# Stage one of a fused token-mixing kernel: three fp32r products in place of one fp32 product, with transfers that convert and add

## The reference, cut to what matters

```python
h = einsum('bhid,oi,od->bho', x, weighted_sum, weight)   # stage one: x is (4, 512, 256, 4)
h = concatenate([h, txt], axis=1)                        # 512 + 77 rows of 256 per batch
xn = layernorm(h)
hid = relu(xn @ gate_w1 + gate_b1); gate = sigmoid(hid @ gate_w2 + gate_b2)
glob = gate * (xn @ U_w) * cumsum(xn @ V_w, axis=1)
h = h + conv3(xn, conv_w) + glob @ out_w + out_b         # conv3: three taps along the rows
y = layernorm(h)
q = round(y / (absmax(y)/127)); qr = round(rhs / (absmax(rhs)/127))
h = h + (q @ qr) * scales                                # int8 product, exact in bf16
```

## Time and profile before

| | |
|---|---|
| three runs | 127.47 us median (126.95 to 129.34) |
| profiled execution, its own time | 126.82 us |
| its span, first to last instruction | 125.0 us |
| mean granted TensorE clock | 0.983 |

### The profile page before, as it was taken

The page is one execution under the profiler, slowest core; times in us unless marked ns, Lnnn a source line. Parts: engine busy times, 40 slices in busy tenths (PEclk is TensorE's granted clock), DMA queues, the critical chain, the costliest instruction groups (busy, mean ns, idle before and its releaser), DMA issues.

```text
span 125.0 us, 1954 instructions
## 1 busy us (share of the span) xinstructions
PE 113.8 (91%) x612; PEld 92.6 (74%) x612; DVE 83.3 (67%) x258; ACT 60.6 (49%) x132; POOL 49.5 (40%) x91
## 2 busy tenths in 40 slices
PE   6999999999999999999889999998996379999960
PEld 5678887687886986888478868866783267999830
DVE  0443431857449688867969898599689948548862
ACT  1300456644814395566048491934484856342520
POOL 2000430022002556362546737360947364554740
PEclk9999999999999999999999999999999959999998
DMA  3899999980000000000012000002021002111014
GB/s 85 237 360 336 423 419 419 419 341 13 0 0 0 0 5 0 3 0 0 33 50 84 5 28 0 0 0 87 0 84 30 0 0 84 39 45 30 3 36 157
DMA packets 5307, 12.05 MB, mean 96 GB/s; under 512 B 456, under 2 KB 3632, under 8 KB 4529
## 3 DMA queue, kind: packets, MB, share of 16 engines
q1 hardware_dynamic: 4721, 11.27, 24.5%
q10 hardware_dynamic: 576, 0.66, 1.7%
HBM read 9.52 MB, written 2.41 MB: 95 GB/s over the span
## 4 chain that ended last, share of the span: by engine, by line
PE 78%; DVE 13%; ACT 3%; issue 2%; POOL 1%; POOLq 0%; ACTq 0%; DVEq 0%
PE h_ps L720 42%; PE uvg_ps L778 5%; PE xt_ps L847 4%; PE h_ps L806 4%; PE h_ps L810 4%; DVE csum L601 3%; PE qt_ps L829 3%; DVE convT L613 3%; PE acc_ps L840 3%; DVE tmp L679 2%; PE uvg_ps L785 2%; DVE stats L552 2%; PE h_ps L816 2%; PE xt_ps L764 2%; ACT qT L488 1%
## 5 line engine op out<-in xcount | busy, mean ns | idle before, releaser
L720 PE MATMUL h_ps<-w_tok,x_sb 128*128 128x256 f32 x256 | 64.2, 394 | 0.0
L720 PEld LDWEIGHTS h_ps<-w_tok,x_sb 128*128 128x128 f32 x256 | 48.0, 197 | 9.5 <-issue 3.6
L552 DVE BATCH_NORM_STATS2 stats<-h_ps 128x6 f32<-128x256 f32 (+1 forms) x36 | 13.9, 423 | 13.9 <-PE h_ps L816 7.8
L341 POOL TENSOR_SCALAR rstd<-mv 128x2 f32<-128x2 f32 (+2 forms) x21 | 4.8, 227 | 37.4 <-DVE mv L555 36.7
L379 POOL TENSOR_SCALAR v<-xc,qmul 128x256 f32<-128x256 f32 (+1 forms) x20 | 10.6, 538 | 16.0 <-DVE qmul L657 15.8
L342 POOL TENSOR_TENSOR rstd<-rstd,exponent 128x2 f32<-128x2 f32 (+2 forms) x21 | 15.0, 713 | 1.8
L481 ACT ACTIVATE glob<-glob 32x256 fp32r<-32x256 f32 (+1 forms) x16 | 7.2, 448 | 11.9 <-POOL glob L353 6.3
L505 ACT ACTIVATE xc<-h_ps,nmean 128x256 f32<-128x256 f32 (+1 forms) x20 | 8.6, 470 | 8.9 <-DVE nmean L629 8.9
L353 POOL TENSOR_TENSOR glob<-gate,us 32x256 f32<-32x256 f32 x8 | 6.6, 831 | 14.7 <-ACT gate L472 14.7
L495 ACT ACTIVATE xn<-h_ps,shift,rstd 128x256 f32<-128x256 f32 x16 | 8.2, 564 | 8.7 <-DVE shift L641 8.6
L391 POOL TENSOR_TENSOR fin<-tmp,h 128x512 f32<-128x512 f32 (+1 forms) x10 | 11.0, 1100 | 0.5 <-DVE tmp L679 0.5
(11 more groups left out here) (89 smaller groups left out, 147.5 us busy)
## 6 DMA issues: line engine op xcount, KB each, us to landing
x_sb<-x_dram SPq DMA_DIRECT2D x6, 1024.0 KB, 16.1
out_dram<-fin SPq DMA_DIRECT2D x8, 256.0 KB
x_sb<-x_dram SPq DMA_DIRECT2D x2, 512.0 KB, 8.5
x_sb<-x_dram SPq DMA_DIRECT2D x2, 256.0 KB, 5.7
txt_sb<-txt_dram SPq DMA_DIRECT2D x1, 308.0 KB
out_dram<-fin SPq DMA_DIRECT2D x4, 77.0 KB
par_sb<-par_dram SPq DMA_DIRECT2D x1, 277.0 KB, 9.1
ws_sb<-ws_dram ACTq DMA_DIRECT2D x2, 128.0 KB, 4.2
```

What stands on the lines that cost most here:

```text
L552: last = nc.vector.bn_stats(stats[0:rows, t, :], src(t))
L720: last = nc.tensor.matmul(h_of(g)[:, t, :], x_sb[:, g, kc, t * P:(t + 1) * P], w_tok[:, kc, :], start=(kc == 0 and t == 0), stop=(kc == KC ...
```

## The change

Groups 0 and 1 stay as they are. For groups 2 to 7 a k step is six fp32r matmuls of 128 x 256: high part of x times high part of w, high x times low w, low x times high w, for each half of the rows. The high part of x comes from a transfer that GpSimd issues and that converts fp32 to fp32r; ScalarE copies its negative into `x_low`; a second GpSimd transfer adds x to that in place. Both are in halves of 512 KB, so each group takes four transfers and two copies. Three buffers go round. `w_high` is made by ScalarE, `w_low` by VectorE. The first loads are spread anew over the SyncE and ScalarE queues, x of group 0 has its own layout, and w's rows are spread by eight transposes in place of four matmuls. `nmean` goes: `centre` makes the negative of the centred value from the mean directly; `scale` loses its use of `rstd2`, which a product in `out` takes in.

```diff
+PLAIN = 2
+RING = 3
+HIGH_AT = {2: 0, 3: 0, 4: 0, 5: 25, 6: 33, 7: 41}
+NEGATE_AT = {2: (0, 1), 3: (9, 11), 4: (20, 22), 5: (30, 32), 6: (38, 40), 7: (46, 48)}
...
-WARM_FIRST = 3
+WARM_FIRST = 4
...
-            eng.dma_start(x_sb[:, g, k, :], x[g, :, k, :]).then_inc(x_loaded[g][n], 16)
+            src = x[g - 1, :, k, :] if g else x0[k, :, :].rearrange("k p t -> p k t")
+            eng.dma_start(x_sb[:, g, k, :], src).then_inc(x_loaded[g][n], 16)
...
+        HALF_KC = [slice(0, KC // 2), slice(KC // 2, KC)]
+
+        def turn_of(g):
+            return 16 * ((g - PLAIN) // RING + 1)
...
-            sp.dma_start(wt_sb[:, :], wt).then_inc(wt_loaded, 16)
-            load_x(sp, 0, 0)
-            load_x(sp, 0, 2)
-            load_x(sp, 0, 4)
+            for n in range(len(LOADS[0]) - 1):
+                load_x(sp, 0, n)
             load_x(sp, 1, 0)
             sp.dma_start(txt_sb[:, :, :], txt.rearrange("b t d -> t b d")).then_inc(txt_loaded, 16)
             load_x(sp, 1, 1)
             sp.dma_start(par_sb[:, :], par).then_inc(par_loaded, 16)
             sp.dma_start(rhs_sb[:, :, :], rhs).then_inc(rhs_loaded, 16)
-            for g in range(2, GROUPS):
-                load_x(sp, g, 0)
...
+            def load_high(g):
+                if g == PLAIN:
+                    pool.wait_ge(x_loaded[1][1], 16)
+                if g >= PLAIN + RING:
+                    pool.wait_ge(tok_done, g - RING + 1)
+                for n, k in enumerate(HALF_KC):
+                    nc.gpsimd.dma_start(x_high[:, g % RING, k, :], x[g - 1, :, k, :]).then_inc(high_loaded[g % RING][n],
+                                                                                            16)
+
+            def add_x(g, n):
+                pool.wait_ge(negated, 2 * (g - PLAIN) + n + 1)
+                nc.gpsimd.dma_start(x_low[:, g % RING, HALF_KC[n], :], x[g - 1, :, HALF_KC[n], :],
+                                    accum_op=ALU.add).then_inc(low_ready[g % RING][n], 16)
+
             for tick in range(TICKS):
+                for g in range(PLAIN, GROUPS):
+                    if tick == HIGH_AT[g]:
+                        load_high(g)
+                for g in range(PLAIN, GROUPS):
+                    for n in range(2):
+                        if tick == NEGATE_AT[g][n] + 1:
+                            add_x(g, n)
...
-            act.dma_start(ws_sb[:, 0, :], ws[:, 0, :]).then_inc(ws_loaded[0], 16)
-            load_x(act, 0, 1)
-            load_x(act, 0, 3)
-            act.dma_start(ws_sb[:, 1, :], ws[:, 1, :]).then_inc(ws_loaded[1], 16)
-
+            act.dma_start(wt_sb[:, :], wt).then_inc(wt_loaded, 16)
+            for c in range(CB):
+                act.dma_start(ws_sb[:, c, :], ws[:, c, :]).then_inc(ws_loaded[c], 16)
+            act.wait_ge(x_loaded[0][-1], 16)
             act.wait_ge(ones_ready, 1)
...
+            for n, k in enumerate(HALF_KC):
+                act.wait_ge(w_tok_ready, (n + 1) * KC // 2)
+                nc.scalar.activation(w_high[:, k, :], w_tok[:, k, :], ACT.Copy).then_inc(w_high_ready, 1)
+
+            def negate(g, n):
+                act.wait_ge(high_loaded[g % RING][n], turn_of(g))
+                if g >= PLAIN + RING:
+                    act.wait_ge(tok_done, g - RING + 1)
+                nc.scalar.activation(x_low[:, g % RING, HALF_KC[n], :], x_high[:, g % RING, HALF_KC[n], :], ACT.Copy,
+                                     scale=-1.0).then_inc(negated, 1)
...
-                    act.wait_ge(nmean2_ready, j + 1)
+                    act.wait_ge(var2_ready, j + 1)
...
-                                                    ACT.Identity, bias=nmean2[0:rows, j, t:t + 1])
+                                                    ACT.Identity, scale=-1.0, bias=mv2[0:rows, j, t, 0:1])
...
+                for g in range(PLAIN, GROUPS):
+                    for n in range(2):
+                        if tick == NEGATE_AT[g][n]:
+                            negate(g, n)
...
+            for n, k in enumerate(HALF_KC):
+                dve.wait_ge(w_high_ready, n + 1)
+                nc.vector.tensor_tensor(w_low[:, k, :], w_tok[:, k, :], w_high[:, k, :].bitcast(F32),
+                                        ALU.subtract).then_inc(w_low_ready, 1)
...
-                    dve.wait_ge(var2_ready, j + 1)
-                    nc.vector.tensor_scalar(nmean2[0:rows, j, 0:nt], mv2[0:rows, j, 0:nt, 0], -1.0, None,
-                                            ALU.mult).then_inc(nmean2_ready, 1)
...
-                    dve.wait_ge(rstd2_ready, j + 1)
-                    for t in range(nt):
-                        last = nc.vector.tensor_scalar(ls[:, t:t + 1], a[:, t:t + 1], rs[:, t:t + 1], SCALE_FLOOR,
-                                                       ALU.mult, ALU.max)
-                    then_wait(last)
-                    then_wait(nc.vector.reciprocal(a, ls))
-                    nc.vector.scalar_tensor_tensor(out=qm, in0=a, scalar=INT8_MAX, in1=rs, op0=ALU.mult,
-                                                   op1=ALU.mult).then_inc(qmul_ready, 1)
+                    then_wait(nc.vector.tensor_scalar(am, a, SCALE_FLOOR * LN_EPS ** 0.5, -1.0 / INT8_MAX,
+                                                      ALU.max, ALU.mult))
+                    nc.vector.reciprocal(qm, am).then_inc(qmul_ready, 1)
...
+                    dve.wait_ge(rstd2_ready, j + 1)
+                    then_wait(nc.vector.tensor_tensor(lscale[0:rows, j, 0:nt], nstep[0:rows, j, 0:nt],
+                                                      rstd2[0:rows, j, 0:nt], ALU.mult))
...
+                    if kc % (KC // 2) == 0:
+                        pe.wait_ge(high_loaded[g % RING][kc // (KC // 2)], turn_of(g))
+                        pe.wait_ge(low_ready[g % RING][kc // (KC // 2)], turn_of(g))
+                    if g == PLAIN and kc == 0:
+                        pe.wait_ge(w_high_ready, 2)
+                        pe.wait_ge(w_low_ready, 2)
+                    for t in range(2):
+                        at = slice(t * P, (t + 1) * P)
+                        nc.tensor.matmul(h_of(g)[:, t, :], x_high[:, g % RING, kc, at], w_high[:, kc, :],
+                                         start=(kc == 0 and t == 0), stop=False, skip_group_check=True)
+                        nc.tensor.matmul(h_of(g)[:, t, :], x_high[:, g % RING, kc, at], w_low[:, kc, :],
+                                         start=False, stop=False, skip_group_check=True)
+                        last = nc.tensor.matmul(h_of(g)[:, t, :], x_low[:, g % RING, kc, at], w_high[:, kc, :],
+                                                start=False, stop=(kc == KC - 1), skip_group_check=True)
...
+            pe.wait_ge(ident_ready, 1)
             pe.wait_ge(wt_loaded, 16)
             for d in range(ND):
-                nc.tensor.matmul(wt_ps[d], ones[0:1, 0:P], wt_sb[:, d * D:(d + 1) * D], start=True, stop=True).then_inc(wt_spread, 1)
+                for c in range(CB):
+                    n = d * CB + c
+                    last = nc.tensor.transpose(wt_ps[d][:, c * P:(c + 1) * P],
+                                               wt_sb[:, n:n + 1].broadcast_to([P, P]), ident[:, :])
+                last.then_inc(wt_spread, 1)
...
-        "x": xl,
+        "x0": f(xl[0].transpose(1, 0, 2)),
+        "x": f(xl[1:]),
         "ws": by_block(f(f(L0_tok_weighted_sum).T)),
-        "wt": f(f(L0_tok_weight).T).reshape(1, ND * D),
+        "wt": f(f(L0_tok_weight).T.reshape(ND * CB, P).T),
```

More of the change, by code:

```diff
@@ L41, with early_fusion_kernel @@
               sigmoid=14)
+PLAIN = 2
+RING = 3
+HIGH_AT = {2: 0, 3: 0, 4: 0, 5: 25, 6: 33, 7: 41}
+NEGATE_AT = {2: (0, 1), 3: (9, 11), 4: (20, 22), 5: (30, 32), 6: (38, 40), 7: (46, 48)}
 RHS_AT = dict(round=11, turn=17, out=21)
-WARM_FIRST = 3
+WARM_FIRST = 4
 WARM_FROM = 8
 WARM_LAST = (1, 1, 1, 2, 2, 0, 2, 5, 7, 0, 2, 1, 1, 1)
-def early_fusion_kernel(nc, x, ws, wt, txt, par, rhs, out, B, HI, T, D, ND, GH, R):
+def early_fusion_kernel(nc, x0, x, ws, wt, txt, par, rhs, out, B, HI, T, D, ND, GH, R):
     CB = D // P
@@ L115, in sem @@
             return ctx.enter_context(nc.semaphore(name))
-        x_sb = sb("x_sb", [P, GROUPS, KC, PAIR])
+        x_sb = sb("x_sb", [P, PLAIN, KC, PAIR])
+        x_high = sb("x_high", [P, RING, KC, PAIR], F32R)
+        x_low = sb("x_low", [P, RING, KC, PAIR], F32R)
         ws_sb = sb("ws_sb", [P, CB, D])
-        wt_sb = sb("wt_sb", [1, ND * D])
+        wt_sb = sb("wt_sb", [P, ND * CB])
         w_tok = sb("w_tok", [P, KC, D])
+        w_high = sb("w_high", [P, KC, D], F32R)
+        w_low = sb("w_low", [P, KC, D], F32R)
         txt_sb = sb("txt_sb", [T, B, D])
@@ L156, in early_fusion_kernel @@
         rstd2 = sb("rstd2", [P, ITEMS, 2])
-        nmean2 = sb("nmean2", [P, ITEMS, 2])
         amax = sb("amax", [P, ITEMS, 2])
+        nstep = sb("nstep", [P, ITEMS, 2])
         lscale = sb("lscale", [P, ITEMS, 2])
@@ L221, in early_fusion_kernel @@
```

(28 more changed lines are left out.)

## The result

The changed kernel takes **133.0 us** (median of 4 runs, 132.1 to 133.9) against 127.7 (4 runs, 127.0 to 129.3) for the kernel before. The ratio is 1.045, 95% interval 1.041 to 1.050: slower, where 127.8 and a range of 121.5 to 133 were forecast. Medians in this text are over all runs of a kernel; the ratios leave out disturbed runs (lower granted clock, over 1.5% above the kernel's fastest), and the traces of pool_only and best_p3 are of such runs. The profiled execution took 133.65 us (span 131.8), 6.8 more than the 126.82 of before.

What follows compares the result with a forecast made beforehand. Middle bounded by TensorE's matmuls and, four ticks per batch, VectorE's run. Profiled 126.82 + 6.6 (start) - 5.6 (middle) - 0.7 (end) = 127.1, median 0.65 above: 127.8 us; range 121.5 to 133, the forecast's own 125 to 130.5.

Steps and rivals of the forecast that it cites:

- Stage one and VectorE's part: Middle: passes of 0.116 us save 8.1 us over 48 k steps; VectorE's unshortened run takes back 2.0.
- For both engines together I let 0.5 us come through: Middle: ScalarE's twelve copies and GpSimd's 24 transfer issues, set against those engines' idle time, cost 0.5 us (0 to 3).
- The start: Before the text rows, new work in three queues delays the text's turn by 5.1 us; slow clock adds 1.5: +6.6.
- First term, the transfer: Start: the second half of group 2's high part lands at about 17.5 us; the text turns at 23.6.
- Rival 3: Converting and adding transfers at half rate delay the text's turn to 25.7; about 131 us on the median; chance 0.09.
- Second term, from the turn to F: From the text's turn to the first `hidden` product: matmuls on a slow clock after TensorE's wait cost 1.5 us.
- The new loads and transposes, costed at nothing: Start: all that the new first loads and eight transposes gain is lost in the text wait; counted as nothing.
- The end: Behind the last group: the shorter chain without `nmean` and with fewer scale instructions gives -0.7 us (-0.3 to -1.2).
- High and low parts never waited for: Sign in the middle: TensorE never waits for x's high or low parts after group 2.
- the other signs in the middle: Six records a k step in 0.70 us; twelve copies of 1.05 us.
- rival 2: GpSimd's issues at 1.4 us each, ahead of the text rstd and at ticks 33 and 41: median 133.5; chance 0.20.

Runs made afterwards that it cites:

- pool_only: The changed kernel with only GpSimd's two add issues of group 2 moved behind the text's rstd; median 132.26 us, ratio 1.031.
- best_p3: The changed kernel with groups 0 to 2 plain, the start reordered, copies and adds at other ticks; 123.36 us, ratio 0.967 to the kernel before.
- best_p3a: As best_p3, with group 6's adds issued at the start of their tick on GpSimd, ahead of the gating product; 121.76 us, ratio 0.956.
- experiments 6 and 7: The changed kernel with one queue altered: pool_only, then VectorE's w_low split moved behind the text's statistics and shift; ratios 1.031 and 1.048.
- experiment 1: The changed kernel with high loads, group 2's adds and copies, weight rounding and split, and tap_diag moved behind the text's rstd, shift or norm; 128.75 us, ratio 1.013.
- experiment 8: The changed kernel with middle placements altered: adds at the end of their tick, copies of groups 5 to 7 at other ticks; ratio 1.046.
- best_p2: As best_p3, but group 2 is in three products too, its copies right behind the text's norm; 125.06 us, ratio 0.984.
- no_low: The changed kernel without negated copies and adding transfers; the third product multiplies the high parts again; 126.95 us, ratio 0.996.
- experiment 5: The changed kernel with 48 products of ones put before TensorE's wait for the text's norm to keep its clock up; 131.61 us, ratio 1.036.
- experiment 2: The changed kernel without the three products: all groups plain, keeping the new first loads, the eight transposes and the shorter scale chain; ratio 1.003.
- experiment 9: The run of best_p3: the changed kernel with three plain groups, the start reordered, copies and adds at other ticks; 123.36 us, ratio 0.967.

## Why the prediction was wrong

**Stage one and VectorE's part: right.** 0.117 us a pass against 0.116. Before the mixing TensorE waits 1.50 + 0.20 and 1.23 + 0.20 us in the second and third batch, where it waited 0.55 + 0.20 before, and 0.2 in the first: 1.8 us more, forecast 2.0. Most of it is a wait for `out` (L728) and only 0.20 for the taps, which the prediction held for the whole. M without the low part shrinks by 5.4 us, where the prediction had 8.1 - 2.0 = 6.1. In that trace VectorE's waits are 1.6 us more than before, so 8.1 - 1.6 - 5.4 = 1.1 us of the passes' gain is missing; the slower first pass behind another kind of product (0.1 to 0.18 us more) may be it, and no run took it apart.

**"For both engines together I let 0.5 us come through": the step that failed in the middle.** It was 2.6 us (M 63.30 against 60.68), 0.6 of it ScalarE's copies and 2.0 the adds. The durations were right (1.06 and 0.92 us against 1.05 and 0.9). What failed was to price them against idle time of the engine as a whole. Their places in the queue were ahead of an item's rstd and rounding, which the chain of the trace after goes through. best_p3 and best_p3a show it: with group 5's copies at ticks 21 and 22, where no item is under way, the first stretch of 12.09 us takes 10.9, as without any low part, and TensorE's wait of 0.35 us for the rounding is gone from it. The second, which keeps group 7's copies and adds, takes 11.5.

**The start: the mechanism held, two terms were too small.** The queues stood in the order forecast, and experiments 6 and 7 show that GpSimd's adds or VectorE's split moved alone give back little or nothing, while experiment 1, which moved all three, clears the stall to 3.2 us; no run moved two of them. First term, the transfer: the second half of x's high part, forecast for 17.5, released the copy at 19.62, and the text turned at 25.73 instead of 23.6. About half of that is the release, x of group 1: the first issue came at 13.82 instead of 12.7 (12.8 to 14.4 in the seven traces with this start). The other half is the time from the first issue to the landing of the second half, 5.8 us instead of 4.8. In experiment 8's trace, with the same start, the first issue came at 12.81, the second half still took 5.7, and the text turned at 24.66; so the forecast missed by 1 us, and another 1 us wandered. Neither the four loads issued behind nor a slow conversion is the cause: in best_p2 only these two pieces were issued at first, and the second landed after 5.8 us, too; a pair in no_low with no other transfer beside it took 5.4. Rival 3 has the 25.7, but by transfers at half speed, and the converting loads moved 383 GB/s. Second term, from the turn to F: +2.8 instead of +1.5. By experiment 5 the slow clock is 2.1 of it (1.5 against experiment 8's trace). At a full clock 0.7 stays, 0.48 of it the wait behind group 3's copy, which the slow clock hides, as the prediction said. Sum of the start +10.0 instead of +6.6. The new loads and transposes, costed at nothing, were worth nothing (experiment 2).

**The end: -0.4 for -0.7.** The prediction's own terms add up to -0.6. Either is within what the clock does there by itself (below).

**The chances.** "High and low parts never waited for" held in this kernel. So did the other signs in the middle (0.70 us a k step, copies of 1.06 us). The forecast's own range ended at 130.5; rival 2 reached 133.5 by an issue price of 1.4 us, but the price was 0.58 for a load and 0.92 for an add, and the 2.0 us came from where they stood. That a time near rival 2's was measured says nothing for its mechanism. Misses of 3.4 and 2.8 us from two separate steps went the same way, and the range was drawn as if one of them at most would.

The Trainium skill's page "Collectives: The Full Stack", section on why ReduceScatter is half of AllGather, has adding transfers at half rate because they read two sources. The traces agree on the rate: adding transfers that follow each other moved 210 GB/s in experiment 1, against 383 for the same pieces without the add and 419 for plain ones. It was hidden for most groups. In experiment 9 an add issued at 62.83 us landed at 68.27, 5.4 us later, for a k step due at 67.1; a converting load of that trace took 4.1 at best, so the wait of 1.3 us is about what the add takes longer. By the Trainium skill's page "TensorE: Matmul & The Clock Gate", section "Back-to-back issue gap", the k step was estimated at 0.655 us; at 0.70 the trace does not agree, and the measurement decides.

## What to carry to other kernels

Work given to an engine with idle time costs what stands behind it at that place in its queue, not its own duration; ask at each place who waits for the next instruction, and look for ticks in which the answer is nobody. The same kinds of work at other ticks, with one group fewer split (10 copies and 20 issues instead of 12 and 24), turned 4.5% slower into 4.4% faster, nearly all of it at the start. When three queues in a row hold one result, clearing one of them shows little or nothing. Price a transfer from its issue to its landing and not by its bytes alone: a converting load of 512 KB that moves in 1.25 us at 419 GB/s landed 4.1 us after its issue at best, and the adds issued behind four other loads at the start took 9.0 and 10.2 us.
